# State-space block and top-2 experts on one core: two PSUM banks read by one instruction, and expert rows transposed between the layers

## What is computed

```python
x = _layernorm(x + _L0_attn_ref(x, ...))      # returns x + scale * x_out, so 2x + scale * x_out is normed
x = _layernorm(x + _L0_ffn_ref(x, ...))
# _L0_attn_ref
xn = x * rsqrt(mean(x*x) + 1e-6) * norm_w
x_branch, gate = split(xn @ W_in.T)           # 512 channels each
xc = causal_conv4(x_branch) + conv_b;  xc = xc * sigmoid(xc)
dt = soft_clamp(softplus(xc @ W_dt.T + b_dt), 0.001, 0.1, 0.5)
Bp, Cp = xc @ W_B.T, xc @ W_C.T               # 16 states
# scan over 1024 steps, h is 512 x 16 for each of 8 sequences:
h = h * exp(soft_clamp(dt * A)) + dt * Bp * xc
h = h * min(20 / norm(h), 1) at every t divisible by 10;  y = h @ C + D * xc
x_out = (y * gate * sigmoid(gate)) @ W_out.T
# _L0_ffn_ref: 8192 tokens, 8 experts, top 2, 768 places for an expert
h = relu(expert_in @ w1 + b1);  expert_out = h @ w2 + b2
y = sum over the 2 experts of gate * expert_out[expert, place]
```

## Time and profile before

| what | value |
|---|---|
| median of three runs | 2,886.46 us |
| profiled execution, its own time | 2,887.04 us |
| its span, first to last instruction | 2,885.2 us |
| busy: PE, DVE, ACT, POOL | 92%, 84%, 79%, 75% of the span |
| mean granted TensorE clock | 0.971 |

### The profile page before, as it was taken

One profiled execution on the slowest core, in us unless ns is written; L12 is line 12 of the kernel. 1 busy time (PEld: TensorE's weight loads), 2 busy tenths in 40 slices (PEclk: granted clock), 3 DMA queues, 4 the chain that ended last, 5 costly groups with the idle time before them and its releaser, 6 DMA issues. The chain is left out here.

```text
span 2885.2 us, 51759 instructions
## 1 busy us (share of the span) xinstructions
PE 2642.1 (92%) x16812; PEld 2403.8 (83%) x16812; DVE 2434.5 (84%) x3452; ACT 2274.4 (79%) x5161; POOL 2155.9 (75%) x2239
## 2 busy tenths in 40 slices
PE   5899999999999999999999999999999884899992
PEld 4899999999999999999999999999999874576761
DVE  1999999999999999999999999999999986112113
ACT  6999999999999999999999999999999922111113
POOL 1788888888888888888888888888888862423315
PEclk8999999999999999999999999999999986999996
DMA  1222222222222222222232222222222212323216
GB/s 59 67 75 79 78 71 79 78 69 82 71 80 77 75 76 78 73 80 70 77 81 72 79 77 75 77 78 73 80 70 79 72 51 85 81 59 99 60 43 244
DMA packets 153973, 225.73 MB, mean 78 GB/s; under 512 B 46056, under 2 KB 92776, under 8 KB 152552
## 3 DMA queue, kind: packets, MB, share of 16 engines
q1 hardware_dynamic: 131208, 188.98, 22.3%
q0 software_dynamic: 9216, 12.59, 2.5%
q10 hardware_dynamic: 13280, 20.86, 2.1%
HBM read 189.26 MB, written 33.05 MB: 77 GB/s over the span
## 5 line engine op out<-in xcount | busy, mean ns | idle before, releaser
L642 POOL TENSOR_TENSOR H<-H,CB 128x640 f32<-128x640 f32 x832 | 1236.1, 1499 | 224.0 <-DVE H L479 223.9
L479 DVE TENSOR_TENSOR_SCAN H<-DA,PM 128x704 f32<-128x704 f32 x832 | 1317.1, 1604 | 1.3 <-ACT DA L276 1.3
L394 ACT ACTIVATE DA<-DT,SM 128x160 f32<-128x160 f32 x3328 | 1115.9, 424 | 1.5 <-POOL DT L610 0.3
L664 PE MATMUL YB<-H,ID 128*128 128x160 f32 x6656 | 1050.5, 310 | 0.2 <-POOL H L642 0.2
L664 PEld LDWEIGHTS YB<-H,ID 128*128 128x128 f32 x6656 | 989.0, 192 | 16.4 <-issue 11.2
L454 DVE TENSOR_TENSOR PM<-PM,BB 128x640 f32<-128x640 f32 x832 | 678.7, 816 | 5.8 <-DMA BB<-Bd 0.7
L276 ACT ACTIVATE DA<-DA 128x2560 f32<-128x2560 f32 x208 | 485.4, 2334 | 1.7
L1121 POOL DMA_INDIRECT YA<-YS,IG x48 | 75.2, 1566 | 239.9 <-ACT YS L944 228.4
L621 POOL TENSOR_TENSOR FC<-SN,HALF 128x4 f32<-128x4 f32 x206 | 212.4, 1031 | 31.2 <-DVE SN L485 23.2
L765 PE MATMUL PZ<-WO,Z 128*80 128x256 f32 x832 | 188.5, 380 | 0.1
L1177 PE MATMUL PE<-XTE,W 128*128 128x384 f32 x512 | 169.1, 492 | 10.1 <-issue 9.2
(11 more groups left out here) (164 smaller groups left out, 3993.7 us busy)
## 6 DMA issues: line engine op xcount, KB each, us to landing
BB<-Bd SPq DMA_DIRECT2D x208, 320.0 KB, 3.4
CB<-Cd SPq DMA_DIRECT2D x208, 320.0 KB, 3.3
W<-in_w ACTq DMA_DIRECT2D x16, 1024.0 KB
XT<-in_xT SPq DMA_DIRECT2D x52, 160.0 KB, 2.2
XR<-in_xp SPq DMA_DIRECT2D x416, 20.0 KB
X2d<-VV SPq DMA_DIRECT2D x416, 20.0 KB
YA<-VV SPq DMA_DIRECT2D x416, 20.0 KB
HI<-YA SPq DMA_DIRECT2D x6, 1024.0 KB, 9.9
```

What stands on the lines that cost most here:

```text
L394: eng.activation(DA[:, c0:c0 + 2, :, a, m, 1:11].rearrange("p c b t -> p b c t"), DT[:, j % 2, a].rearrange("p b (c t) -> p b c t", c=2), ...
L479: eng.tensor_tensor_scan(H[:, q % 3, u], a0, DBX(u), 0.0, ALU.mult, ALU.add).then_inc(s_scan, 1)
L642: eng.tensor_tensor(h, h, cb, ALU.mult).then_inc(s_hc, 1)
L664: mm = eng.matmul(yv, ID[:], hv[:, :, :, n, 0:10], start=False, stop=n == 15)
```

## The change

In phase 1, PA and PZ become the halves of one PSUM tensor, and `BOTH` is a view of 320 columns of each. The copy to XB, the conv's tanh, XC, the gate's tanh and SG become one instruction each over 640 elements; their semaphores count once for a block, and every wait on them is rewritten for that. The gate's halves change places: columns 512 to 767 now go to PA, 768 to 1023 to PZ. In phase 2, the one-hot work goes in eighths of 8 token columns; XT gets a second buffer; the transposes of expert e + 1 and their copies stand between the layers of expert e; layer 1 starts when two of the three copies are there; and the closing norm's rows are shared 6, 1, 1 between ACT, POOL and DVE (4, 2, 2 in the last batch).

```diff
-        PA = ctx.enter_context(nc.psum_tensor("PA", [128, 512], F32))
-        PZ = ctx.enter_context(nc.psum_tensor("PZ", [128, 512], F32))
+        PAZ = ctx.enter_context(nc.psum_tensor("PAZ", [128, 1024], F32))
+        PA, PZ = PAZ[:, 0:512], PAZ[:, 512:1024]
+        BOTH = PAZ[:].rearrange("p (m n) -> p m n", m=2)[:, :, 0:320]
...
# ACT, slot 1
-                        for m, p in enumerate((PA, PZ)):
-                            eng.wait_ge(s_br, 2 * j + m + 1)
-                            if m == 0 and j > 0:
-                                eng.wait_ge(s_halo, j)
-                            eng.activation(XB[:, 2 * m:2 * m + 2, :, 3:23],
-                                           p[:, 0:320].rearrange("p (a b t) -> p a b t", a=2, b=8),
-                                           ACT.Copy).then_inc(s_xb, 1)
+                        eng.wait_ge(s_br, 2 * j + 2)
+                        if j > 0:
+                            eng.wait_ge(s_halo, j)
+                        eng.activation(XB[:, :, :, 3:23].rearrange("p (m a) b t -> p m (a b) t", m=2),
+                                       BOTH.rearrange("p m (n t) -> p m n t", t=20), ACT.Copy).then_inc(s_xb, 1)
# ACT, slot 5
+                        eng.wait_ge(s_cv, 2 * (j + 1))
+                        if ok(i + 3):
+                            eng.wait_ge(s_ssum, j + 2)
+                        eng.activation(TB[:].rearrange("p (m a) b t -> p m (a b t)", m=2), BOTH, ACT.Tanh).then_inc(s_th, 1)
...
# ACT, slots 13 and 14 (now 14 alone)
-                    if s in (13, 14) and ok(i + 1):
+                    if s == 14 and ok(i + 1):
                         j = i + 1
-                        n, p, m = (0, PA, 1) if s == 13 else (1, PZ, 0)
-                        eng.wait_ge(s_gt, 2 * j + n + 1)
-                        if n == 0 and ok(i + 2):
-                            eng.wait_ge(s_xc, 2 * j + 4)
+                        eng.wait_ge(s_gt, 2 * (j + 1))
+                        if ok(i + 2):
+                            eng.wait_ge(s_xc, j + 2)
+                        eng.activation(TB[:].rearrange("p (m a) b t -> p m (a b t)", m=2), BOTH, ACT.Tanh,
+                                       scale=0.5).then_inc(s_tg, 1)
# DVE, slot 6
+                        eng.wait_ge(s_th, j + 1)
+                        if j >= 2:
+                            eng.wait_ge(s_dtp, 2 * (j - 1))
+                            eng.wait_ge(s_dx, j - 1)
+                        eng.scalar_tensor_tensor(
+                            XC[:, j % 2].rearrange("p (m a) b t -> p m (a b t)", m=2),
+                            TB[:].rearrange("p (m a) b t -> p m (a b t)", m=2), 1.0, BOTH,
+                            ALU.add, ALU.mult).then_inc(s_xc, 1)
# DVE, slot 15
+                        eng.wait_ge(s_tg, j + 1)
+                        if j >= 2:
+                            eng.wait_ge(s_z, 4 * (j - 1))
+                        eng.scalar_tensor_tensor(
+                            SG[:, j % 2, :, :, 1:21].rearrange("p (m a) b t -> p m (a b) t", m=2),
+                            TB[:].rearrange("p (m a) b t -> p m (a b) t", m=2), 1.0,
+                            BOTH.rearrange("p m (n t) -> p m n t", t=20), ALU.add, ALU.mult).then_inc(s_sg, 1)
...
# PE, slots 12 and 13
-                        project(j, 768, PA).then_inc(s_gt, 1)
+                        project(j, 512, PA).then_inc(s_gt, 1)
...
-                        project(j, 512, PZ).then_inc(s_gt, 1)
+                        project(j, 768, PZ).then_inc(s_gt, 1)
...
# phase 2
-        XT = sb("XTE", [128, 2, 768])
+        XT = sb("XTE", [128, 2, 2, 768])
...
-        LO = sb("LO", [128, 2, 2, 16, 128])
+        LO = sb("LO", [128, 2, 2, 8, 128])
...
+        def hidden(e, m, h):
+            return 3 + 22 * e + 2 * m + h
+
+        def turned(e, c):
+            return c if e == 0 else 22 * e - 3 + c
+
+        def result(e, c):
+            return 22 * (e + 1) + c
+
+        def shares(b):
+            return (6, 7) if b < B - 1 else (4, 6)
...
# DVE, PE, ACT and POOL: one-hot work
-            for c in range(4):
-                j = slice(16 * c, 16 * c + 16)
+            for c in range(8):
+                j = slice(8 * c, 8 * c + 8)
...
# DVE, experts
+            def turn(e):
+                if e >= E:
+                    return
+                if e >= 2:
+                    eng.wait_ge(s_h, 16 * (e - 1))
                 for c in range(3):
                     eng.wait_ge(s_xt, 3 * e + c + 1)
+                    eng.tensor_copy(XT[:, e % 2, :, 256 * c:256 * c + 256],
+                                    bank(turned(e, c))[:].rearrange("p (a n) -> p a n", a=2)).then_inc(s_xtc, 1)
+
+            turn(0)
+            for e in range(E):
                 for m in range(8):
...
+                turn(e + 1)
                 for c in range(3):
...
# DVE, closing norm, after the statistics of batch b + 1
+            def normed(b):
+                eng.wait_ge(s_nm, b + 1)
+                for j in range(shares(b)[1], 8):
+                    eng.tensor_scalar(rows(b)[:, j], rows(b)[:, j], SD[:, b, j:j + 1], NM[:, b, j:j + 1],
+                                      ALU.mult, ALU.add).then_inc(s_x3v, 1)
...
# PE, experts
+            turn(0)
+            for e in range(E):
                 eng.wait_ge(s_wl[e % 2], 32 * (e // 2 + 1))
-                eng.wait_ge(s_xtc, 3 * (e + 1))
+                eng.wait_ge(s_xtc, 3 * e + 2)
                 for m in range(8):
                     for h in range(2):
+                        n = hidden(e, m, h)
+                        if (m, h) == (0, 1):
+                            eng.wait_ge(s_xtc, 3 * e + 3)
...
+                turn(e + 1)
                 eng.wait_ge(s_hr, 8 * (e + 1))
                 eng.wait_ge(s_hv, 8 * (e + 1))
```

More of the change, by code:

```diff
@@ L154, in ssm_phase @@
         users_pz = [
-            (2, s_xb, lambda j: 2 * j + 2),
-            (2, s_xc, lambda j: 2 * j + 1),
+            (2, s_xb, lambda j: j + 1),
+            (2, s_xc, lambda j: j + 1),
             (2, s_bcs, lambda j: 4 * j + 4),
             (-1, s_v, lambda j: j + 1),
-            (1, s_sg, lambda j: 2 * j + 2),
+            (1, s_sg, lambda j: j + 1),
         ]
@@ L438, in dt_x @@
                 eng.wait_ge(s_dt, j + 1)
-                eng.wait_ge(s_xc, 2 * (j + 1))
+                eng.wait_ge(s_xc, j + 1)
                 if c >= 2:
@@ L937, in scalar_program @@
                         eng.wait_ge(s_y, 3 * e)
-                    eng.activation(HT[:, m, 0:384], bank(22 * e + 3 + 2 * m)[:, 0:384], ACT.Relu,
+                    eng.activation(HT[:, m, 0:384], bank(hidden(e, m, 0))[:, 0:384], ACT.Relu,
                                    bias=B1[:, e, m:m + 1]).then_inc(s_hr, 1)
@@ L949, in scalar_program @@
                 x = rows(b)
-                for j in range(5):
+                for j in range(shares(b)[0]):
                     eng.activation(x[:, j], x[:, j], ACT.Identity, bias=NM[:, b, j:j + 1],
@@ L1135, in gpsimd_program @@
                 eng.wait_ge(s_nm, b + 1)
-                for j in range(5, 8):
+                for j in range(*shares(b)):
                     eng.tensor_scalar(x[:, j], x[:, j], SD[:, b, j:j + 1], NM[:, b, j:j + 1],
@@ L1151, in tensor_program, with turn @@
                     eng.wait_ge(s_gate[n], c + 1)
-                    for j in range(16):
-                        t = eng.matmul(GP, LO[:, c % 2, n, j], HI[:, n, 16 * c + j], start=(c, n, j) == (0, 1, 0),
-                                       stop=(c, n, j) == (3, 0, 15))
+                    for j in range(8):
+                        t = eng.matmul(GP, LO[:, c % 2, n, j], HI[:, n, 8 * c + j], start=(c, n, j) == (0, 1, 0),
+                                       stop=(c, n, j) == (7, 0, 7))
                     t.then_inc(s_gi, 1)
             eng.wait_ge(s_rt, RT_IX)
-            for e in range(E):
-                k = 22 * e
+            def turn(e):
+                if e >= E:
+                    return
                 for c in range(3):
-                    if k + c >= 8:
-                        done, n = evacuated(k + c - 8)
-                        eng.wait_ge(done, n)
+                    n = turned(e, c)
+                    if n >= 8:
+                        eng.wait_ge(*evacuated(n - 8))
                     eng.wait_ge(s_xe[e % 2][c], 32 * (e // 2 + 1))
```

111 lines of the change are left out of this document (44 added, 67 removed).

## The result

The changed kernel takes **2,855.31 us** (median of 4 runs, 2,853.67 to 2,856.99) against 2,886.42 us for the kernel before, timed beside it (4 runs, 2,884.79 to 2,888.19): a ratio of 0.9892, interval 0.9875 to 0.9909. That is 31.1 us less. The forecast was 2,863 with a range down to 2,856: the sign and the order of the parts were right, and the gain of 31.1 us was larger than the 23.3 forecast and 0.7 us beyond the end of the range. The profiled execution took 2,855.47 us (span 2,853.7, mean granted clock 0.973).

The account below looks back on a forecast made before the run. DVE bounds the long first phase, PE the expert phase, POOL and DMA closely the closing norm. Terms -2.0 - 1.5 - 15.3 - 4.5 = -23.3 us gave 2,863 us, range 2,856 to 2,872.

Parts of the forecast that it names:

- part 1: Phase 1, two PSUM banks read as one: 4.0 us gained, 2.0 us lost in the fill, -2.0 us in all.
- part 3: Experts, transposes between the layers: 2.07 us gone for each of 7 experts, 0.8 for the first, -15.3 us (-16.5 to -11).
- The fill: Start of phase 1, where DVE waits for ACT: longer merged instructions lose 2.0 us (1 to 3).
- The steady term: Phase 1 where DVE is the bound: some 100 merged pairs save 0.04 us each, 4.0 us gained.
- ACT's later readers: Phase 1 blocks: ACT falls back about 0.5 us, covered by its 0.91 us of waiting for DVE; costed at nothing.
- Part 2: One-hot work in eighths: only the head start before PE's 256 instructions shrinks, -1.5 us (-2.5 to +1).
- Part 4: Closing norm's rows shared out: last row ready 5.7 us earlier, output transfer 4.6 at best, -4.5 us (-6 to -1).
- (a): Phase 1: product L442 collides with POOL's XN product and ends about 0.66 us later, 34 us, 2,897 in all; 4%.
- (b): Experts' borders: gaps return because gather, relu or bank release ends late; half of part 3 stays, 2,870; 6%.
- (c): Phase 1: merged instructions give nothing, ACT's lateness reaches DVE, 0.3 us in each of 50 blocks, 2,882; 3%.
- (d): Closing norm: Part 4 is held by DMA already, only 1 us gained, 2,867; 12%.
- (e): Phase 1: a removed DVE instruction saves 0.14 us and not 0.04, 10 us more, 2,853; 4%.

Follow-up runs that it names:

- e5: The kernel after with one more wait, stopping PE before an expert's layer 1 until DVE has added the last expert's bias: 2,864.67 us.
- e6: The kernel after with each block's second dt*x product (L442) issued behind the scan of slot 4 instead of before it: 2,825.82 us, ratio 0.9783.

## Why the prediction was right, and where it failed

The forecast had the mechanisms and the order of the parts right, and failed by two sizes, both too small: in part 1 the duration taken for the merged DVE instruction, in part 3 the price of a stand of PE. The drain's 2.1 us came on top by luck.

**Part 1, -2.0 forecast.** The fill was right: +2.14 in the first comparison, 2.1 by the medians, against 2.0. The steady term was mis-sized: 0.04 us for each pair, 4.0 us in all, with an end of 5; it measured 6.3 us, 0.064 us for each of the 98 pairs of the 49 steady periods, in after and, within 0.2 us, with the banks alone. The step that failed is the duration taken for the merged instruction: 0.74 us came from the product with B (L454), another operation with as many elements, and the merged one takes 0.71 from start to start. The bound rested on the rounding of the starts alone, as if the two operations were known to cost the same. The Trainium skill ("VectorE: DVE Perf Modes", the section on the TRN2 errata) gives an instruction with a PSUM source a fixed 120 cycles, 125 ns, which would have made it, as an estimate from that page, 12.5 us. The durations in the trace agree with it, 0.93 us for a pair and 0.79 for the merged one; what the stream gains does not, since neighbouring instructions overlap by 0.08 us (0.79 us long, 0.71 apart), and 0.064 of the 0.14 us is left. ACT's later readers were covered, as forecast: the wait for DVE fell by 0.54 us, about the 0.5 that was worked out.

**Part 2, -1.5 forecast.** Right, 1.7. The comparison gave what was said, and a POOL product fell to 0.83 us where 0.94 was estimated from another product's size.

**Part 3, -15.3 forecast, end -16.5.** Every interval named there is gone, and the experts alone gained 17.4 to 18.5 us; the 1.1 us between the two lie in the first one's layer 1, which ran at different granted clocks. The step that failed is the price of a stand, for which the term counted PE's idle time alone. What was left out is the longer stream behind each stand: 20.88 and 20.96 us before, 20.64 and 20.72 after. There are 14 such stands fewer, 14 x 0.24 = 3.4 us, and 14.5 + 3.4 = 17.9, which is what the chain shows from the end of the first expert's layer 1 on (338.28 and 320.46 us, 17.8 less). e5 shows that a stand of 0.97 us costs 1.21 to 1.23. The part before the first layer was 1.0 instead of 0.8.

**Part 4, -4.5 forecast.** Right, 4.9 to 5.0. A DVE row costs 0.30 us in the chain and the period is 3.59, as estimated (0.3 and 3.57), and the DMA engines are full until 2.7 us before the end. The transfer decides, as said: counted from the arrival of the first batch, the last row is ready 5.9 us earlier than before (5.7 forecast) and the end comes 4.6 us earlier (4.6 forecast); the other 0.3 us lie ahead of that arrival.

**The sum.** The steady term (2.3 us), the experts (2.9) and small ones of 0.25 us or less in routing, head start, first layer and 0.4 in the tail make 6.3 of the 8.2 us between the 23.3 forecast and the 31.5 found between the spans; 2.1 are the scatter of the drain, and the fill took 0.1 back. The low end of the range was 0.7 us too high. With equal drains the two spans would lie 29.4 us apart, which is inside the range, so that the time fell outside it is in part chance; that two terms were too small is not. The ends of parts 1 and 3 were both passed, because each was set from what the estimate already contained, rounding there and the visible idle time here. Both terms were priced from something near the thing itself: another operation of equal size, and the idle time without the start behind it.

**The rivals.** (a), the collision with XN, did not come: L442 stayed at 0.48 us beside XN, with the start 0.01 us before it. Its mechanism was nonetheless real and already being paid elsewhere in each block, for 1.12 us against 0.49, a number that stood in the forecast's list of signs and was never asked about; e6 shows it is worth 31 us. The Trainium skill ("SBUF — State Buffer", "SBUF: two separate sides") has an exclusive lock on a port pair, held for the whole instruction by whichever starts first. The runs agree for a DVE product that comes 0.7 us into a running product of POOL: it ends 0.36 us after it. They do not agree for recorded starts 0.07 us apart, where the later one went first. That the lock lies in the port pair was not measured by itself. (b) did not come: no stand at the borders. (c) did not come: DVE waits for ACT nowhere in the 800 us. (d) did not come: the tail gained 4.9 us and not 1. (e), 0.14 us for a removed instruction, is refuted by 0.064; 0.14 is the difference of the durations, of which the overlap takes the rest.

## What to carry to other kernels

On an engine that is full, price an instruction by the distance to the next start in the stream, taken from the same operation, and a stand by its idle time plus the overlap that it destroys (here 0.16 + 0.07 us for a fp32 matmul of 384 columns). Where the same instruction shows two durations in one trace, find out what runs beside the longer one before anything else: here that was worth as much as the whole change. And compare stretches between milestones rather than whole times, since a kernel that scatters over 5 us has stretches that repeat to 0.8 us in 2,160; but take stretches in which the granted clock is not 1.00 from several executions.

## What the runs showed of the hardware

- A DVE product with both operands in SBUF (128x320, fp32) that starts inside a running POOL product waits for it: 1.12 us instead of 0.49, ending 0.36 us behind it. POOL's running product keeps its time, and its next one then takes 1.74 us instead of 1.48. Where the two start within 0.1 us of each other, DVE's keeps its 0.49 us and POOL's is stretched (from 0.86 to 1.18 to 1.28 us), even where POOL's start is recorded 0.07 us earlier.
- A merged instruction over two PSUM banks shows no charge for the step. On DVE 320 more elements cost 0.31 to 0.33 us (0.79 against 0.46 to 0.48), twice what 160 more cost within a bank (0.46 to 0.48 against 0.30, though that is another operation, L498); on ACT they cost 0.27 us (0.68 to 0.72 against 0.41 to 0.45), as between the rows.
- In a full DVE stream each of these instructions starts the next one 0.08 us before its own end, so a removed one saved 0.064 us and not the 0.14 by which the durations differ.
- A fp32 matmul stream of 64 takes 20.64 us when entered without a stop and 20.88 behind a stand of 0.97 us, at the same granted clock of 1.00.
- At the end of the state-space phase, with gaps between PE's groups of matmuls, the granted clock differs between executions of one kernel, and 32 equal matmuls take 4.88 us at 1.00 and 7.41 at 0.62.
